# Constant products on TensorE in thirty idle places of a four-layer model kernel

## The reference

```python
def _layernorm(x, axis=-1, eps=1e-05):
    m = jnp.mean(x, axis=axis, keepdims=True)
    v = jnp.var(x, axis=axis, keepdims=True)
    return (x - m) / jnp.sqrt(v + eps)
...
    x = _layernorm(x + _L0_attn_ref(x, ...), axis=-1)  # attention in windows of 32 tokens, 16 heads
    x = _layernorm(x + _L0_ffn_ref(x, ...), axis=-1)   # 16 experts, 4 chosen by sigmoid scores in groups, and a shared one
    x = _layernorm(x + _L1_attn_ref(x, ...), axis=-1)  # 8 heads, 3-wide queries and keys with fixed directions
    x = _layernorm(x + _L1_ffn_ref(x, ...), axis=-1)   # 8 experts, 2 chosen, with a capacity for each
    x = _layernorm(x + _L2_attn_ref(x, ...), axis=-1)  # rotary attention, 8 heads of 128
    x = _layernorm(x + _L2_ffn_ref(x, ...), axis=-1)   # rotary attention with 16 heads of 64, then 31 experts, 3 chosen
    x = _layernorm(x + _L3_attn_ref(x, ...), axis=-1)  # gated linear recurrence, then a gated MLP
    x = _layernorm(x + _L3_ffn_ref(x, ...), axis=-1)   # router with a hidden layer, 8 experts, 2 chosen, and a shared one
```

## Time and profile before

| | us |
|---|---|
| median of 3 runs (lowest, highest) | 1852.05 (1846.07, 1853.19) |
| the profiled execution, its own time | 1846.22 |
| span of its records | 1844.4 |
| TensorE matmul busy | 1554.3 (84%) |
| TensorE weight load busy | 1002.0 (54%) |
| VectorE busy | 1031.4 (56%) |
| ScalarE busy | 1004.5 (54%) |
| GpSimd busy | 767.2 (42%) |
| mean granted TensorE clock, of full speed | 0.914 |

### The profile page before, as it was taken

One profiled execution on the slowest core, in us unless ns is written; L12 is line 12 of the kernel. 1 busy time (PEld: TensorE's weight loads), 2 busy tenths in 40 slices (PEclk: granted clock), 3 DMA queues, 4 the chain that ended last, 5 costly groups with the idle time before them and its releaser, 6 DMA issues. The chain is left out here.

```text
span 1844.4 us, 27071 instructions
## 1 busy us (share of the span) xinstructions
PE 1554.3 (84%) x8739; PEld 1002.0 (54%) x8756; DVE 1031.4 (56%) x2126; ACT 1004.5 (54%) x2164; POOL 767.2 (42%) x712
## 2 busy tenths in 40 slices
PE   5658978860877899999789999999989999868898
PEld 3337643330874566666445555555448886323685
DVE  5956675631213655555355555555548886662575
ACT  4324554550423455555556656565538887664686
POOL 1224530027352566666264555545324443022263
PEclk8979977975887999999899999999979999979799
DMA  1008210021223222222211111111027652000330
GB/s 41 1 14 183 62 82 23 1 95 42 80 61 114 45 61 58 58 58 58 70 46 46 36 47 38 44 43 39 24 62 266 228 209 95 1 0 21 123 122 25
DMA packets 62165, 125.50 MB, mean 68 GB/s; under 512 B 14354, under 2 KB 29571, under 8 KB 55532
## 3 DMA queue, kind: packets, MB, share of 16 engines
q1 hardware_dynamic: 59724, 119.57, 22.2%
q0 software_dynamic: 2304, 4.24, 0.7%
HBM read 79.39 MB, written 11.35 MB: 49 GB/s over the span
## 5 line engine op out<-in xcount | busy, mean ns | idle before, releaser
L1852 ACT ACTIVATE h_probs<-psum,h_nmax 128x512 f32<-128x512 f32 (+3 forms) x256 | 132.7, 523 | 132.4 <-DVE h_nmax L1932 77.8
L1932 DVE TENSOR_REDUCE h_nmax<-psum 128x1 f32<-128x512 f32 (+3 forms) x256 | 113.5, 486 | 118.3 <-PE psum L1742 118.3
L1667 POOL TENSOR_TENSOR h_swapped<-h_swapped,rope_tables 128x512 f32<-128x512 f32 x64 | 81.9, 1280 | 158.4 <-DMA h_swapped<-h_raw 158.4
L897 ACT ACTIVATE psum<-psum,f_b 128x512 f32<-128x512 f32 x200 | 131.8, 659 | 27.8 <-PE psum L857 27.8
L823 POOL TENSOR_TENSOR e_lo<-e_gated,e_hi 128x512 fp32r<-128x512 f32 x59 | 76.1, 1290 | 148.1 <-ACT e_hi L909 148.1
L1852 ACT ACTIVATE a_probs<-psum,a_nmax 128x512 f32<-128x512 f32 (+3 forms) x128 | 67.6, 528 | 123.8 <-DVE a_nmax L1932 75.6
L1667 POOL TENSOR_TENSOR a_swapped<-a_swapped,a2f_a_tables 128x512 f32<-128x512 f32 x64 | 82.3, 1286 | 126.1 <-DMA a_swapped<-a_raw 125.9
L932 DVE TENSOR_TENSOR e_lo<-psum,e_hi 128x512 fp32r<-128x512 f32 x168 | 114.7, 683 | 26.4 <-ACT psum L897 26.4
L1739 PE MATMUL psum<-h_k,h_q 64*128 64x384 f32 (+3 forms) x512 | 104.9, 485 | 20.6 <-DVE h_p_t L1941 16.8
L855 PE MATMUL psum<-f_x_hi,f_w_hi 128*128 128x512 f32 x272 | 109.0, 401 | 5.8 <-DVE e_gated L946 3.9
L1749 PE MATMUL psum<-ident,h_probs 128*128 128x128 f32 x640 | 108.7, 277 | 0.4 <-ACT h_probs L1852 0.4
(11 more groups left out here) (471 smaller groups left out, 4074.6 us busy)
## 6 DMA issues: line engine op xcount, KB each, us to landing
e_gate<-gates SPq DMA_DIRECT2D x39, 1024.0 KB, 4.8
a_swapped<-a_raw SPq DMA_DIRECT2D x128, 128.0 KB, 2.3
h_swapped<-h_raw SPq DMA_DIRECT2D x256, 64.0 KB, 2.0
e_gate<-gates SPq DMA_DIRECT2D x16, 512.0 KB, 7.4
f_w<-in_l_experts SPq DMA_DIRECT2D x17, 256.0 KB, 4.9
f_w<-in_l_experts SPq DMA_DIRECT2D x32, 128.0 KB, 4.7
slots<-a_empty SPq DMA_DIRECT2D x1, 2600.0 KB, 7.5
e_got<-slots SPq DMA_DIRECT2D x8, 325.0 KB, 5.5
```

Source lines behind the costliest of these rows:

```text
L897: nc.scalar.activation(to, hidden_bank(n), ex.act_func, **bias(n)).then_inc(act_ready, 1)
L1667: nc.gpsimd.tensor_tensor(swapped[:, j, :], swapped[:, j, :], tables[:, 2 * j + 1, :], ALU.mult).then_inc(sin_ready, 1)
L1852: nc.scalar.activation(probs[:, j % 4, 0:(q + 1) * P], ring[j % RING][:, 0:(q + 1) * P], ACT.Exp, bias=nmax[:, j % 8:j % 8 + 1], accum_out ...
L1932: nc.vector.tensor_reduce(nmax[:, j % 8:j % 8 + 1], ring[j % RING][:, 0:(q + 1) * P], AX.X, ALU.max, negate=True).then_inc(max_ready, 1)
```

## The change

A new function, `keep_busy`, issues n products of two constants (`mean_w`, 128 x 128, by 256 columns of `rope_tables`) into the first half of a PSUM bank that holds nothing at that time. Nobody reads the result. It is called at 25 places of the code, some of which run in several stages; 214 such products are executed. In `capacity_experts` a new semaphore lets TensorE wait until GpSimd has issued 28 of its 32 scatters, and in `rope_attention` and `direction_scores` a wait on an existing semaphore stands ahead of the products.

```diff
+def keep_busy(core, pe, bank, n):
+
+    for _ in range(n):
+        core.nc.tensor.matmul(core.psum[:, bank, 0:T // 2], core.mean_w[:], core.rope_tables[:, 0, 0:T // 2], start=True, stop=True)
@@ Head.tensor @@
+        if not first.center:
+            keep_busy(self.core, pe, 7, 3)
         for b in range(B + 2):
@@ window_attention @@
                     if not last:
                         front(c + 1)
+                    else:
+                        keep_busy(core, pe, 7, 12)
                     values(c, first, last)
+                    if last:
+                        keep_busy(core, pe, 0, 5)
...
                 out(B - 1)
+                keep_busy(core, pe, 0, 2)
@@ experts @@
+                if not ex.gate_output:
+                    keep_busy(core, pe, 0, 4)
                 for n in range(ahead):
                     hidden(n)
                 for n in range(n_items):
...
+                keep_busy(core, pe, 0, 3)
@@ router @@
+                keep_busy(core, pe, 3, 20 if kind == "sigmoid_groups" else 7 if hidden else 0)
                 pe.wait_ge(gates_ready, 1)
@@ capacity_router @@
+                keep_busy(core, pe, 3, 10)
                 pe.wait_ge(chosen_ready, 1)
@@ capacity_experts @@
+                    if t == NT - 3:
+                        pool.sem_inc(nearly_sent, 1)
...
+                pe.wait_ge(nearly_sent, 1)
+                keep_busy(core, pe, 0, 16)
                 turn(0)
...
                 output(E - 1, 1)
+                keep_busy(core, pe, 0, 16)
                 for b in range(B):
                     pe.wait_ge(home_loaded[b], 2 * 16)
...
+                keep_busy(core, pe, 4, 3)
@@ rope_attention @@
+                    if U == 0 and slot in (3, 4, 5, 7):
+                        keep_busy(core, pe, 7, 2)
...
                 head.tensor(pe)
+                keep_busy(core, pe, 6, 5)
                 for V in range(AHEAD):
                     project_q(V)
...
+                pe.wait_ge(raw_ready[1], AHEAD)
+                keep_busy(core, pe, 6, 10 if merged else 4)
                 scores(0)
...
+                keep_busy(core, pe, 0, 3)
@@ direction_scores @@
+                pe.wait_ge(rest_ready, len(items) - 3)
+                keep_busy(core, pe, 0, 5)
@@ direction_attention @@
+                keep_busy(core, pe, 2, 3)
                 pe.wait_ge(mask_ready, 1)
...
                     first_products(f, m_read)
+                    keep_busy(core, pe, 3, 1)
...
                 m_read = q_ready, 1
+                keep_busy(core, pe, 3, 3)
                 second(0)
...
+                keep_busy(core, pe, 2, 3)
                 spread_sums(n_units - 1, m_read)
+                keep_busy(core, pe, 2, 5)
                 out(B - 1, (ln_ready, n_units))
+                keep_busy(core, pe, 2, 3)
@@ recurrence @@
                 z_gate(0)
+                keep_busy(core, pe, 4, 7)
                 z_conv(1)
...
+                keep_busy(core, pe, 2, 18)
                 out(0)
...
+                keep_busy(core, pe, 5, 3)
```

More of the change, by code:

```diff
@@ L1397, in capacity_experts @@
         hid = st.sb("hid", [P, 2, HT, CAPACITY])
-        (sent, turned, x_rounded, x_split, hid_psum, hid_ready, out_psum, out_ready, returned, joined) = (st.sem(n) for n in (
-            "sent", "turned", "x_rounded", "x_split", "hid_psum", "hid_ready", "out_psum", "out_ready", "returned", "joined"))
+        (sent, nearly_sent, turned, x_rounded, x_split, hid_psum, hid_ready, out_psum, out_ready, returned, joined) = (st.sem(n) for n in (
+            "sent", "nearly_sent", "turned", "x_rounded", "x_split", "hid_psum", "hid_ready", "out_psum", "out_ready", "returned", "joined"))
         got_loaded = [st.sem(f"got{e}_loaded") for e in range(E)]
```

## The result

The changed kernel takes 1833.59 us (median of 4 runs, 1823.84 to 1838.80) against 1852.62 before: a ratio of 0.9896, with a 95% interval from 0.9866 to 0.9925. That is 19 us faster; 27.6 us less and 1824 were forecast, with a range of 1804 to 1846.

A forecast was written before the change was run, and what follows sets the result against it. The prediction took TensorE's half-clock stretches, mostly at joints (316.0 us, TensorE busy 182.9), as the whole prize. Its gains and costs by part summed to 27.6 us less, forecasting 1824 us, with a range of 1804 to 1846.

The forecast's parts named there:

- Norm starts, +9.3: Seven norms after stage changes: clock held, 1.65 us gained each, 11.6 in all, times 0.8 since some fall anyway.
- Stage ends, -4.1: Three products at stage ends make the barrier come 0.59 us later at seven ends: 4.1 us lost.
- Direction attention, +2.4 and +0.4: First unit, serial steps and VectorE's waits gain, less 2.2 us for products: net 2.4; its tail gains 0.4.
- heads over 2 us apart: Sign of being wrong: heads in direction attention this far apart mean half clock with a product each.
- the third rival: Slower: constants do not raise or hold the clock and products outlast their cover; 43 us lost, 1895; chance 0.05.
- Capacity experts, +2.3 and +0.8, and capacity router, +1.0: Sixteen products behind the 28th scatter gain 2.3 us, sixteen before the join 0.8, ten behind the router's transposes 1.0.
- Experts of ffn2, +1.8, and second rope attention, +1.6: ffn2: 3.4 us gained less 1.7 for four products; second rope: half-clock stretches recovered, less 1.9 for eight products.
- First rope attention, +2.0: Half of 6.15 us is 3.1; eight products in unit 0 cost 3.4, two thirds hidden in idle gaps.
- The other joints: Window attention's tail gains 1.9 us, first router and experts 1.8, recurrence 2.5, last router and experts 1.8.
- The first rival: The clock falls again in what is left of the waits: 9 us gain, 1843; chance 0.14.
- The second (it holds everywhere, 42 us): The clock holds at norms and all joints: 42 us gain, 1810; chance 0.12 for a gain beyond 40.
- The fourth (nothing changes): The joints are bound by ACT, VectorE and DMA: within 5 us of 1852; chance 0.07.

The follow-up runs named there:

- e5: e1 with every constant product on 32 rows instead of 128, same 256 columns streamed; 1856.29 us, ratio 1.002.
- e2: The changed kernel with only the products at stage ends and three at the head of the norm without centring; 1847.93 us, ratio 0.9970.
- e1: The changed kernel without the products in the first part of direction attention (entry, seven heads, before `second(0)`); 1827.34 us, ratio 0.9864.
- e8: e1 without 60 products in four long waits (capacity router, before the transposes, before the join, before `out(0)`); 1826.06 us, ratio 0.9842.
- e6: e1 with the capacity experts' release hung on a GpSimd memset and 28 products instead of 16 before the join; 1824.72 us, ratio 0.9840.
- e9: e6 without e7's removals and the capacity router's ten; 17 products instead of 10 before first rope scores, 28 instead of 18 before `out(0)`; 1818.38 us.
- e7: e1 without the four products before the first expert and the eight in each rope attention's unit 0; 1825.97 us, ratio 0.9837.
- e10: e1 with every constant product on 64 rows; 1842.17 us, ratio 0.9943.

## Why the prediction was right, and where its sum was wrong

The forecast was faster by 27.6 us, and it is 19. The mechanism stands: with e5 the clock's part can be told from the products' own, and e2 gives the barriers' part as forecast. That the time lies well inside the range owes something to luck: half of the sum was put on three stretches that in the traces gave nothing, and the wide range took that in.

*Norm starts, +9.3.* Right, a little small. The seven norms gained 11.3 us in the changed kernel's trace. My factor of 0.8 for norms that would fall again was not needed; none did.

*Stage ends, -4.1.* Right: 0.56 us at a barrier against 0.59 worked out, and with the norms 5.2 forecast against e2's 5.6.

*The price of a product, 0.43 and 0.86.* Right, and with it the heads' 2.75 us.

*Direction attention, +2.4 and +0.4.* Wrong, and the costliest error. I read "balanced at half clock, VectorE-bound at full" and reckoned that the clock would be up after two heads, so that five of the seven products would be hidden. The clock stayed down through all seven (256.61 to 280.51) with TensorE busy 23.89 of 23.90 us. Unit 0 starts its second products at 284.15 and unit 1 at 299.36, the same 15.2 us as in the earlier trace rows, where I expected 12.9. The loss I took as 2.2 was 6.3 (e1; 6.7 by the traces). I had the row that said so: in the earlier trace rows the clock stays at 0.50 for 41 us from 258.69 with TensorE busy three quarters of the time. And "heads over 2 us apart" was my own sign of failure, priced at 11 us in the third rival. That rival decided this place, at a lower price, and the four products in ffn2 (3.4 by it, 3.2 in the trace); no run shows it anywhere else.

*Capacity experts, +2.3 and +0.8, and capacity router, +1.0.* Wrong. "The new increment stands behind it" was the failing step: the queue of GpSimd executed the increment while its engine still had 12 of the 28 scatters ahead of it to do, 15 us early. The clock was down again when the transposes came, as also behind the other three fillers, and e8 shows no gain from them. With the release mended and the join filled the traces of e6 and e9 are shorter behind the scatters, by an amount that isn't settled.

*Experts of ffn2, +1.8, and second rope attention, +1.6.* Wrong. I put the four products at 1.7 us before a gain of 3.4, but they stand behind the gates' products in which the clock goes, cost 3.2 at half clock and come too late to save it; the experts give about 1.5 of it back. The second rope gave nothing either: from the norm's first scaled block to the sixty-fifth score product it takes 77.3 us in the changed kernel and 76.6 before. Why is not shown. The second norm, put at +2.1, gave 1.3 up to the router's first product.

*First rope attention, +2.0.* Right: the stretch gained 2.6, with the later barrier already in it. Here the eight products in unit 0, which e7 takes out, carry most of the gain.

*The other joints.* Window attention, first router and experts, the recurrence and the last experts gave what was put on them, within the spread of one execution.

The first rival (the clock falls again in what is left of the waits) describes the capacity experts, the router in front of them and `out(0)`, but not the norms. The second (it holds everywhere, 42 us) fails in three stretches, though e9 with 35 us shows that most of that prize is there. The fourth (nothing changes) is out. The Trainium skill (TensorE: Matmul & The Clock Gate, Part 1) calls the ramp under 1% of a typical span. Here, with the products' cost already paid, 1.0% was won back in the changed kernel and 1.9% in e9: as a bound on this gain it did not hold.

## What to carry to other kernels

A product of constants pays where TensorE would be idle right up to the next real work: look at what stands between the last filler and that work, and fill it or leave it empty. It doesn't pay where TensorE has no idle time, even when the clock is down, since it is then paid in full at half speed; read that from brackets that are missing in the timeline, not from a busy share. At the opening of a loop in which the clock keeps falling, a few products can pay, as in the first rope attention. And hang a release in mid-stream on an operation of the engine itself, then look in the trace when it fires.

## What the runs showed of the hardware

- Constant products on 128 rows with 32 columns of weights held the clock as those with 128 did (0.945 and 0.946). With 32 rows the kernel stood at 0.921, with 64 rows at 0.931, against 0.957 with 128 (e5, e10, e1, profiled executions). Two of the kernel's own stretches go with it: the heads, whose scores have operands of 32 rows, run at 0.50 with TensorE busy 23.89 of 23.90 us, and the clock falls to 0.50 2 us into the gates' products of 32*128, behind 0.93 us of idle time. It is no strict rule. e5's 32 rows served as well as 128 in the first rope attention (326.26 and 326.76 us), and among the heads constant products on 128 rows, 1.22 of each 2.75 us, didn't bring the clock back.
- An increment in GpSimd's queue ran ahead of 12 indirect scatters that stand before it in the program, by 15 us (16 scatters of 1.28 us each still follow its time, 442.4, in the trace, where 4 should); a memset with the increment attached ran in its turn.
- The same kernel varies by 15 us between executions with its granted clock (0.946 to 0.957). Where it falls varies too: in the second norm and router of ffn2, on the same code at that place, the router's first product comes at half clock in e1's and e7's traces and at full in those of e6, e8 and the changed kernel, and from there to the gates' product it is 21.3 and 22.0 us or 18.6. One profiled execution of such a kernel can show less than half of what the medians gain.
